# A norm step moved ahead of two pieces of the MLP on VectorE

## The reference, cut to what matters

```
qkv = x @ Wqkv;  q, k, v = split(qkv, 3)            # 16 heads of 64
q = l2norm(q) * qs;  k = l2norm(k) * ksc            # per head: t / max(|t|, 1e-12)
q = rotary(q) * scale;  k = rotary(k) / scale
x = x + local_attention(q, k, v, window=32) @ Wo    # softmax over own and previous window
xn = layernorm(x) * g + bln
a, gate = split(xn @ W1 + b1, 2)                    # DI = 341 each
x = x + (a * gelu(gate)) @ W2 + b2
```

## Time and profile before

| | |
|---|---|
| median of 3 runs | 4350.36 us (4349.73 to 4355.24) |
| profiled execution | 4327.38 us, its span 4325.6 us |
| TensorE busy | 3659.8 us, 85% |
| VectorE busy | 3370.4 us, 78% |
| ScalarE busy | 2655.0 us, 61% |
| GpSimd busy | 2616.9 us, 60% |
| mean granted TensorE clock | 0.919 of full |

### The profile page before, as it was taken

One profiled execution on the slowest core, in us unless ns is written; L12 is line 12 of the kernel. 1 busy time (PEld: TensorE's weight loads), 2 busy tenths in 40 slices (PEclk: granted clock), 3 DMA queues, 4 the chain that ended last, 5 costly groups with the idle time before them and its releaser, 6 DMA issues. The chain is left out here.

```text
span 4325.6 us, 161629 instructions
## 1 busy us (share of the span) xinstructions
PE 3659.8 (85%) x62588; PEld 2579.0 (60%) x62588; DVE 3370.4 (78%) x5230; ACT 2655.0 (61%) x6841; POOL 2616.9 (60%) x2852
## 2 busy tenths in 40 slices
PE   7788989898999999885556678989898889988997
PEld 3466666666666666662111256666666666666664
DVE  7688778777878778766888878878777878778874
ACT  2467667676667667663333356667666767667664
POOL 3476666666666667651444466666666666667662
PEclk9899999999999999997777789999999999999998
DMA  1122232322322222320000022232222222222321
GB/s 36 50 65 70 70 74 65 72 65 68 73 65 71 68 66 70 73 55 14 0 0 0 16 55 68 65 75 67 67 69 66 71 70 69 68 69 66 76 65 40
DMA packets 183110, 252.03 MB, mean 58 GB/s; under 512 B 53658, under 2 KB 74782, under 8 KB 182302
## 3 DMA queue, kind: packets, MB, share of 16 engines
q1 hardware_dynamic: 182422, 241.71, 23.4%
HBM read 39.13 MB, written 1.05 MB: 9 GB/s over the span
## 5 line engine op out<-in xcount | busy, mean ns | idle before, releaser
L835 POOL TENSOR_TENSOR qk_rows<-rot_products 128x512 f32<-128x512 f32 x768 | 982.5, 1279 | 795.8 <-DVE rot_products L642 795.8
L642 DVE TENSOR_TENSOR rot_products<-psum,rot_scaled 128x1024 f32<-128x1024 f32 x768 | 936.7, 1220 | 137.4 <-ACT squares L468 104.7
L843 POOL TENSOR_TENSOR qk_rows<-qk_rows,rnorm 128x512 f32<-128x512 f32 x768 | 813.9, 1091 | 15.0
L267 PE MATMUL psum<-wqkv_hi,xs_hi 128*128 (+1 forms) x1152 | 572.3, 497 | 201.3 <-DVE rot_products L642 147.6
L468 ACT ACTIVATE squares<-psum 128x512 f32<-128x512 f32 x768 | 479.8, 625 | 216.9 <-PE psum L269 201.0
L280 PE MATMUL psum<-ident,qk_rows 128*128 128x128 f32 x3072 | 429.3, 286 | 115.0 <-issue 112.3
L644 DVE TENSOR_REDUCE sumsq<-squares 128x8 f32<-128x512 f32 x768 | 518.9, 676 | 0.0
L364 PEld LDWEIGHTS psum<-o_t,wo 128*128 128x128 f32 x3072 | 445.9, 227 | 81.2 <-ACT o_t L484 68.2
L364 PE MATMUL psum<-o_t,wo 128*128 128x128 f32 x3072 | 460.2, 313 | 27.9 <-ACT o_t L484 26.7
L269 PE MATMUL psum<-wqkv_hi,xs_lo 128*128 (+1 forms) x1152 | 471.8, 410 | 0.0
L268 PE MATMUL psum<-wqkv_lo,xs_hi 128*128 (+1 forms) x1152 | 469.0, 407 | 0.0
(11 more groups left out here) (157 smaller groups left out, 6344.1 us busy)
## 6 DMA issues: line engine op xcount, KB each, us to landing
v_pairs<-v_rows SPq DMA_DIRECT2D x3072, 64.0 KB, 2.0
wqkv_staged<-in_Wqkv SPq DMA_DIRECT2D x52, 384.0 KB, 3.3
wo<-in_Wo SPq DMA_DIRECT2D x12, 512.0 KB, 4.6
w<-in_W SPq DMA_DIRECT2D x12, 341.0 KB, 3.5
qk_scale<-in_qk_scale SPq DMA_DIRECT2D x12, 128.0 KB, 3.4
w<-in_W SPq DMA_DIRECT2D x12, 128.0 KB
rot_base<-in_rot SPq DMA_DIRECT2D x2, 512.0 KB, 3.8
out_x<-qk_rows SPq DMA_DIRECT2D x1, 1024.0 KB, 5.1
```

The source lines that it names most:

```text
L267: nc.tensor.matmul(proj_ps[c % 2], xh, wh, start=True, stop=False)
L642: V.tensor_tensor(m["mm"][:, c % 2, :, :].rearrange("p a (h e) -> p a h e", e=DH), ps, cos_sin, ALU.mult)\
L835: G.tensor_tensor(qk[:, c * CH:(c + 1) * CH].rearrange(half, a=2, e=DH // 2), cos, sin[:, :, ::-1, :], ALU.add)\
L843: G.tensor_tensor(part, part, m["rn"][:, u % 2, HC * c:HC * c + HC].unsqueeze(2) .to_broadcast([P, HC, DH]), ALU.mult).then_inc(S["rot_don ...
```

## The change

In `dve_body`, the order of VectorE within a slot, `dve_rnorm(it, u + 2)` now stands ahead of `dve_hidden(it - 1, 0)` in slot 1 and of `dve_down(it - 1)` in slot 3. In slot 2 the second gated product still comes first, then the norm step, and slot 0 has no piece of the MLP there. No instruction is added or removed, and the written order of the other four engines is the same.

```diff
                 if proj:
                     dve_rotate(layer, j, u + 2, (2, 3))
+                if mlp and u == 2:
+                    dve_hidden(it - 1, 1)
+                if proj:
+                    dve_rnorm(it, u + 2)
                 if mlp and u == 1:
                     dve_hidden(it - 1, 0)
-                if mlp and u == 2:
-                    dve_hidden(it - 1, 1)
                 if mlp and u == 3:
                     dve_down(it - 1)
-                if proj:
-                    dve_rnorm(it, u + 2)
                 if mlp and u == 2:
                     dve_hidden(it - 1, 2)
```

## The result

The changed kernel takes 4441.1 us (median of 4 runs, 4431.9 to 4455.1) against 4350.05 (4 runs, 4340.5 to 4355.2): a ratio of 1.0211, 95% interval 1.0169 to 1.0253. It is 91 us slower. I had forecast slower, but by 14 us, with 4390 as the upper end of the range. The two profiled executions are 107.9 us of span apart (4433.5 against 4325.6). One outcome first: with TensorE's code moved by 160 instructions, the same two kernels differ by nothing that can be measured (experiments 17 and 18).

The account below looks back on a forecast made before the run. TensorE, the busiest engine with few holes, was taken to bound the kernel. Cold slots (0.04 us × 34, 1 us) and warm (1.1 us × 12, 13 us) gave +14 us, 4364.5 us; range 4345 to 4390, the forecast's own 4355 to 4378.

Parts of the forecast that it names:

- The blocked L665: Norm step in slots 1 and 3: L665 waits under GpSimd's addition, 0.78 us; norm step ends 1.93 us after the sum.
- TensorE held at L267 in slots 1 and 3: L267 starts later: 0.2 us in cold slots 1, 1.3 in warm ones, 0.44 in slot 3.
- the relief in slot 2: Slot 2 after a cold slot 1: GpSimd's addition ends earlier, L618 is blocked less; gain 0.4 us, bounds 0 to 0.6.
- the warm slots 1: 12 slots 1 without a gelu wait, TensorE at full clock: L267 1.3 us later, 0.65 left; with slot 3, 13 us.
- the cold ones: 34 slots 1 where VectorE waits for gelu, TensorE partly at 1.2 GHz: L267 0.2 us later, cost 0; total 1 us.
- The direction: Whole kernel: slower, by 14 us or 0.3%; chance of slower 0.60.
- my sum: Whole kernel: cold slots 1 us plus warm slots 13 us, together +14 us.
- rival 4: New holes in warm slots send TensorE to its low clock: +50 us, 4400; chance 0.08.
- covered: Cold slot 1: TensorE's wait for o_t, 0.33 us each, hides the 0.2 us delay; cost 0, or 0.2 without cover.
- GpSimd gets the norm step about 0.85 us earlier: Slot 3: GpSimd's head start of about 0.85 us gains nothing, as TensorE starts L280 after the jump long after.
- the jump's 2.48 us starts when the queue reaches it: Slot 3: no hole between L267 and the jump, so the 0.44 us delay goes wholly into the iteration.
- 0.63 us to spare: Slot 2 after a warm slot 1: late PV delays DMAs and v rows; gelu's slack covers 0.63 of 1.3 us, leaving 0.65.

Follow-up runs that it names:

- experiments 17 and 18: 80 tiny matmuls once, in the layer norm ahead of the first stack: changed kernel 4350.1 us, 1.0027; kernel before 4360.2 us, 1.0049.
- 9 to 11: Two spare GpSimd products in slot 3, added to the slot-3 half alone, the changed kernel with third gelu first, and the kernel before: 1.0091, 1.0152, 0.9985.
- Experiment 3: Changed kernel with ScalarE's third gelu ahead of the v rows in slot 2: 4397.2 us, 1.0111 of the kernel before.
- 15 to 18: 96 tiny matmuls in slot 1 of the changed kernel, third gelu first (1.0386) or not (1.0529); 80 once ahead of the first stack, changed (1.0027), before (1.0049).
- 4: Kernel before with ScalarE's third gelu ahead of the v rows in slot 2: 4345.7 us, 0.9986.
- 6: Kernel before with one spare DMA on SP's queue behind the 16 DMAs: 4336.8 us, 1.0006.
- 8: Kernel before with four of the 16 DMAs issued by ScalarE's queue: 4336.8 us, 0.9995.
- 11: Kernel before with two spare GpSimd products in slot 3: 4343.9 us, 0.9985.

## Why the prediction was right or wrong

**Right.** The blocked L665 (0.76 us, 1.91 in all); TensorE held at L267 in slots 1 and 3; the relief in slot 2, where the wait for L386 fell from 28.2 to 6.3 us. Undisturbed, slot 2 gave back 0.62 us, more than the 0.4 I took and about the bound of 0.6. The holds came out near the forecast or below: 1.23 to 1.33 us in the warm slots 1 (forecast 1.3), 0.12 on average in the cold ones (forecast 0.2), 0.18 on average in slot 3 (forecast 0.44). The direction was right too, but by luck: what made the kernel slower is not in my sum, and at the other place of the blocks it is not slower.

**Slot 1.** I took the cold and warm slots for given, 34 and 12, and 13 of my 14 us stood in the warm ones. Of the 41 slots counted, 31 had some time at the low clock before, and 38 after (rival 4's direction), so 3 warm ones were left. A cold slot 1 took 19.66 us before, a warm one 17.65: seven more cold ones are some 14 us, half of what slot 1 lost (0.69 × 41 = 28 us). That the edit makes them cold is not shown: at the other place there are 38 in the kernel before and 35 in the changed one. I also costed cold slots at 0, "covered" by the wait for o_t. At the other place slot 1 costs +0.40 us. This term was mis-sized, by up to 0.40 × 48 = 19 us; the hold itself is 0.16 of that in a cold slot, and where the rest comes from was not traced.

**Slot 3, the step that failed.** That GpSimd gets the norm step about 0.85 us earlier and nobody waits for it holds (9 to 11). But "the jump's 2.48 us starts when the queue reaches it, so all of it goes into the iteration" took the jump for a constant. Its hole was 2.74 us on average before (112.3 us in 41) and 3.36 after (137.8). Slot 3 cost +0.82, not +0.44, and most of it is this +0.62. The hold of TensorE stands between the last fetch of code and the branch. As I read it, with the hold the fetch behind the loop is asked for before the jump, and the hole is some 4.0 us instead of 2.7.

**Slot 2, the other failed step.** I let PV's delay reach the v rows by its own size, with 0.63 us to spare, and forgot what the 16 DMAs share their engines with. PV of slot 1 came later and TensorE was earlier in slot 2, so a fetch that had followed the last issue by 1.7 us on average moved mostly to 0.4 to 1.7 (1.0 on average), and half the v rows became late by some 2 us. Experiment 3 puts this at about 44 us net.

**The clock.** The time at the low clock rose from 701 us before to 837 after; at the other place it is 731 before and 745 after. So the low clock followed the new holes and was not a cause of its own, but it carries about half of the loss: the 57.5 us by which TensorE's busy time rose. PV behind a late row (3.64 us for 2.07) is an example.

At the other place the edit is worth −6.5 us (−14 to +1). My sum of +14 us is nearer to that than to the +91, but it lies outside the interval, and the sign of what was measured is open. That −6.5 is not the edit by itself either, since the late v rows of slot 3 hide part of it there. The rest, 91 + 6.5 or about 98 us, comes only where TensorE's blocks of code lie as in these two kernels. How the fetches choose their moment was inferred from their order and ends, not measured directly: no run shows which engine a packet belongs to. That the place of TensorE's code decides is shown (15 to 18); that the extra packet is the code behind the loop is the reading that fits all of them.

No kernel tried beats the one before by more than can be measured (4, 6, 8 and 11 are all within their intervals).

## What to carry to other kernels

Before a change of some tenths of a microsecond is judged, look in a tightly bound loop at the packets of code in the DMA view: beside small DMAs that someone waits for, and between the last matmuls and the jump. Run both kernels a second time with the code moved by half a block from outside the loop; if the verdict turns, it was the place and not the edit. A ratio of 1.02 with a tight interval is a fact of two binaries, not yet of two orders of work.

## What the runs showed of the hardware

- TensorE's jump at the end of a loop of 2703 instructions costs a hole of 2.4 to 3.1 us, and some 4.0 (up to 4.6) where one more packet of code runs beside its own (before and after). The branch instruction itself lasts 3.3 to 5.2 us there, and 0.2 us in TensorE's short loops of the other parts (L1050, L1201). ScalarE and GpSimd branch in the same iterations in 0.045 us.
- A 16 KB packet of code beside a DMA of 64 KB from SBUF to SBUF turned 2.0 us to landing into 3.6: the DMA's last three packets came when the packet of code, 1.37 us long, had ended.
- A 64-row bf16 matmul of 8 columns takes about 35 ns with its weight load (80 in 2.8 us, 96 in 3.3), while PV's 128 take 16 ns each at full clock (2.07 us).
